# SyncE opens the first score level ahead of its loads of expert weights, and ScalarE takes a one-column exponential ahead of its wait for the level

## The chip, the core and the metric

The kernel runs on one NeuronCore of a Trainium2 chip. The core has five engines with an instruction stream each: TensorE (PE in the profile; its weight loads are PEld), VectorE (DVE), ScalarE (ACT), GpSimd (POOL) and SyncE (SP), which here issues transfers. The engines meet only through semaphores. The metric is the device time of one execution in microseconds (us), the median of several runs. A second number is the span of the one execution that the hardware profiler recorded.

## The reference, cut to what matters

4096 rows of width 128 pass through four layers, each added to its input: an adjacency attention, a dense mixture of two experts, a second adjacency layer and a mixture of experts with a choice of two experts for each row. The change lies at the start of the third layer:

```python
h = jnp.tanh(input @ W + b)
inp = input @ W
e = (h @ a)[:, 0]
valid = jnp.sum(h, axis=1) != 0
mask = (adj[:M] > 0) & valid[None, :]
scores = jnp.where(mask, e[None, :], neg)
m = jnp.max(scores, axis=1, keepdims=True)
w = jnp.where(mask, jnp.exp(scores - m), 0.0)
att = w / jnp.maximum(jnp.sum(w, axis=1, keepdims=True), 1e-30)
return att @ inp
```

The fourth layer adds, for each row, the two best of eight experts of the form gelu(x W1 + b1) W2 + b2; their weights are the `weights` that the diff mentions.

## The kernel before, in words

There are four functions, `prepare`, `attend`, `mix_and_project` and `gather_and_route`, each with one block in which every engine has its own program. A block ends with a barrier of all five engines. The change lies in the last one, `gather_and_route`, whose block begins at L1381.

`mix_and_project` leaves in SBUF: the scores `e` (32 columns, one per tile of 128 rows), `valid`, the normalized rows `xn`, and `levels`, a number that VectorE works out at L1000 from the spread of the scores. Its last ScalarE instruction is a one-column exponential into a spare column (L1114).

`gather_and_route` computes exp(e - max) in levels: a row of the adjacency whose sum is too small at one level is taken at the next, with all scores lifted by 16. The body of a level is a loop of a runtime count: `levels` (L1366 to L1370) reads the count from SBUF into a register (`value_load`, L1368) and runs `Fori` over it (L1369). Each engine does that for itself. In the profiled execution the body runs once.

The body of a level, `level_of`, exists on each engine and begins with a wait for the semaphore `level_open` to reach the number of the level. SyncE raises `level_open` once ahead of its own `levels` (L1429), and once more at the end of each level (L1427), when all engines have reported that they are done.

- SyncE (L1383 on) first issues five transfers that bring all expert weights into `weights`: W1 (L1385), W2 in two (L1387), b2 (L1389), b1 (L1390). They signal `weights_in`, for which ScalarE waits ahead of the first expert tile (`step_of(0)`, L1644 on), and VectorE after the levels. Then it raises `level_open` (L1429) and enters `levels`. Inside the level its first work waits for `first_table`, which is written after five of the eight chunks.
- VectorE (L1903 on) waits for a column of ones from GpSimd, enters the loop, waits for the level, writes `exponent` (L1906), waits for ScalarE's exponential, scales it (L1913), and makes for each of eight groups `values` (L1769) and the low half of `parts` (L1775).
- ScalarE (L1657 on) waits for the level, then for `exponent`, writes `weight` with the exponential (L1661), and then for each group the high half of `parts` (L1605).
- TensorE waits for the level and then, in chunk 0, for `parts` of each group. Each of the eight chunks is 32 tiles of two matmuls of 512 columns (L1467), with small turns, gates and ranks between the groups.
- GpSimd blanks the ones column (L1701) and two parts of `rows` (L1703), waits for the level, and later scatters rows by indirect DMA (L1713).

The functions that read activation tables are Exp, Tanh and Gelu. The program loads a table in front of the instruction that needs it (ACT_TABLE_LOAD in the trace); the loop body holds an Exp at its beginning and Gelus at its end.

Of the kernel before, what the change touches and what calls it, by code (L numbers as in the profile page):

```python
# [16 lines left out]
ACT = mybir.ActivationFunctionType  # L17
AX = mybir.AxisListType

P = 128  # L20
# [1198 lines left out]
def gather_and_route(nc, io, sb, ps):  # L1219

    with ExitStack() as ctx:
        buf = lambda name, shape, dt=F32: ctx.enter_context(nc.sbuf_tensor(name, shape, dt))
# [10 lines left out]
        values = buf("values", [P, VALUE_SLOTS, SUB, D])  # L1233
        sumsT = buf("sumsT3", [P, GROUP])
        exponent, weight = buf("exponent", [P, TILES]), buf("weight", [P, TILES])
        take, inverse = (buf(n, [P, SUB])[:, :] for n in ("take", "inverse"))
        e, valid, xn, left = sb["e"], sb["valid"], sb["xn"], sb["left"]
        mask = sb["mask"][:, :].bitcast(F8)
# [29 lines left out]
        level_open, level_closed = sem("level_open"), sem("level_closed")  # L1268
# [98 lines left out]
        def levels(eng, body):  # L1367
            count_ = eng.value_load(sb["levels"][0:1, 0:1], min_val=1, max_val=MOST_LEVELS)  # L1368
            with eng.Fori(1, count_ + 1) as level:  # L1369
                body(level)  # L1370
# [3 lines left out]
        def landed_rows(level, chunks, u):  # L1374

            return (level - 1) * (PER_CHUNK * len(range(u, LAST, SLOTS))) + PER_CHUNK * len(range(u, chunks, SLOTS))
# [4 lines left out]
        with nc.Block() as block:  # L1381

            @block.sync  # L1383
            def _(sp):
                sp.dma_start(weights[:, :, 0:F], io["W1b"].rearrange("e d f -> d e f")).then_inc(weights_in, 16)  # L1385
                for f in range(FH):
                    sp.dma_start(weights[:, :, F + f * D:F + (f + 1) * D],  # L1387
                                 io["W2b"].rearrange("e (f p) d -> f p e d", p=P)[f]).then_inc(weights_in, 16)
                sp.dma_start(weights[:, :, 2 * F:2 * F + D], io["b2b"].partition_broadcast(P)).then_inc(weights_in, 16)  # L1389
                sp.dma_start(weights[:, :, 2 * F + D:], io["b1b"].rearrange("e p f -> p e f")).then_inc(weights_in, 16)  # L1390

                def load_rows(k, landed, before):
                    start = sp.value_load(table[0:1, 1, k:k + 1], min_val=0, max_val=E * N + (ROUTED_STEPS - 1) * 2 * P)  # L1393
                    if before:

                        sp.wait_ge(landed, 16 * before)
                    sp.dma_start(sorted_rows[:, k, :, :], io["sorted"][bass.ds(start, 2 * P), :].rearrange("(h p) n -> p h n", p=P))\  # L1397
                        .then_inc(landed, 16)

                def level_of(level):  # L1400
                    sp.wait_ge(level_open, level)
                    sp.sem_inc(entered, 1)
                    sp.wait_ge(first_table, 1)
                    for n in range(SLOTS):
                        sp.wait_ge(scattered[n], landed_rows(level, FIRST_CHUNKS, n))
                        sp.sem_inc(entered, 1)
                    for k in range(FIRST):
                        load_rows(k, rows_in[0][k % LOADS], k // LOADS)
                    sp.wait_ge(second_table, 1)
                    for n in range(SLOTS):  # L1410
                        sp.wait_ge(scattered[n], landed_rows(level, SECOND_CHUNKS, n))
                        sp.sem_inc(entered, 1)
                    for k in range(FIRST, EARLY):
                        load_rows(k, rows_in[0][k % LOADS], k // LOADS)

                    for n in range(SLOTS):
                        sp.wait_ge(scattered[n], landed_rows(level, LAST, n))
                        sp.sem_inc(entered, 1)
                    for u in range(OUTS[0]):
                        sp.wait_ge(y_out[0][u], level * (32 * len(range(u, FIRST, OUTS[0]))))  # L1420
                        sp.sem_inc(entered, 1)
                    for done in level_done.values():
                        sp.wait_ge(done, level)
                        sp.sem_inc(level_closed, 1)
                    for spent in each_level:
                        sp.sem_clear(spent)
                    sp.sem_inc(level_open, 1)  # L1427

                sp.sem_inc(level_open, 1)  # L1429
                levels(sp, level_of)  # L1430

                sp.wait_ge(last_scattered, PER_CHUNK)
                sp.wait_ge(rest_table, 1)
                for k in range(EARLY, ROUTED_STEPS):
                    load_rows(k, rows_in[1][(k - EARLY) % LOADS], (k - EARLY) // LOADS)
                for u in range(OUTS[1]):
                    sp.wait_ge(y_out[1][u], 32 * len(range(u, ROUTED_STEPS - FIRST, OUTS[1])))
                for g in range(GROUPS):
                    u = g % RING
                    if g >= RING:  # L1440
                        sp.wait_ge(mixed_added, g - RING + 1)
                    sp.dma_start(both[:, u, :, :, :], io["mixed"][2 * g * GROUP:2 * (g + 1) * GROUP, :].rearrange("(p c s) d -> p c s d", p=P, c=2))\
                        .then_inc(both_in[u], 16)
                    if g >= RING - 1:
                        store = g - RING + 1
                        sp.wait_ge(mixed_added, store + 1)
                        sp.dma_start(io["out"].rearrange("(t p) d -> p t d", p=P)[:, store * SUB:(store + 1) * SUB, :],
                                     x_tiles[:, store * SUB:(store + 1) * SUB, :]).then_inc(rows_out, 16)
                for store in range(GROUPS - RING + 1, GROUPS):
                    sp.wait_ge(mixed_added, store + 1)  # L1450
                    sp.dma_start(io["out"].rearrange("(t p) d -> p t d", p=P)[:, store * SUB:(store + 1) * SUB, :],
                                 x_tiles[:, store * SUB:(store + 1) * SUB, :]).then_inc(rows_out, 16)
                sp.wait_ge(rows_out, 16 * GROUPS)
# [147 lines left out]
            def _(act):  # L1601

                def keep_high(g):
                    act.wait_ge(values_ready, g + 1)
                    nc.scalar.activation(parts[:, g * SUB:(g + 1) * SUB, 0, :], values[:, g % VALUE_SLOTS, :, :], ACT.Copy,  # L1605
                                         scale=1.0 / PART_SCALE).then_inc(hi_ready, 1)
# [14 lines left out]
                def keep_turned():  # L1621
                    return nc.scalar.activation(xT[:, :], ps[:, TURN_BANK, :], ACT.Copy)
# [30 lines left out]
                def steps(c, *groups):  # L1653
                    for i in steps_at(c, *groups):
                        step_of(i)

                def level_of(level):  # L1657
                    act.wait_ge(level_open, level)
                    act.sem_inc(entered, 1)
                    act.wait_ge(exponent_ready, 1)  # L1660
                    nc.scalar.activation(weight[:, :], exponent[:, :], ACT.Exp).then_inc(exp_ready, 1)  # L1661
                    for g in range(GROUPS):
                        keep_high(g)
                    for c in range(GROUPS):
                        scale_low_sums(c)
                        steps(c + 1, 0, 1, 2)
                        if c == LAST:
                            break
                        act.wait_ge(turned, c + 1)
                        if c:  # L1670

                            act.wait_ge(gates_ready, c)
                        keep_turned().then_inc(xT_ready, 1)
                        steps(c + 1, 3, 4)
                        act.wait_ge(measured, c + 1)
                        if c >= SLOTS:

                            act.wait_ge(scattered[c % SLOTS], landed_rows(level, c, c % SLOTS))
                        stage(c, 0).then_inc(staged, 1)
                        steps(c + 1, 5)  # L1680
                        stage(c, 1).then_inc(staged_again, 1)
                        steps(c + 1, 6, 7)
                    act.wait_ge(staged_again, LAST)
                    act.wait_ge(down_ready[0], FIRST)
                    act.wait_ge(scattered[LAST % SLOTS], landed_rows(level, LAST, LAST % SLOTS))
                    act.sem_inc(level_done["act"], 1)
# [366 lines left out]
```

## Time and profile before

| what | value |
|---|---|
| median of 3 runs | 844.4 us (842.9 to 844.82) |
| the profiled execution's own time | 846.05 us |
| its span | 844.3 us |
| TensorE busy | 703.9 us (83% of the span) |
| VectorE busy | 571.5 us (68%) |
| ScalarE busy | 498.9 us (59%) |
| GpSimd busy | 196.8 us (23%) |
| mean granted TensorE clock | 0.924 of full speed |

Times in rows are us from the start of the span, durations of single instructions in ns. An engine's name with a q (SPq, ACTq) is its sequencer: register, branch, semaphore and DMA-issuing instructions, which are not counted as busy. PEclk is the granted TensorE clock as a share of full speed, 0.50 at 1.2 GHz and 1.00 at 2.4 GHz.

### The profile page before, as it was taken

The page shows a single profiled execution, that of the slowest core. Times are in us where ns is not written, and L with a number is a line of the kernel's source. Part 1 is how long each engine was busy: PE and PEld are TensorE (multiplying, and loading weights), DVE is VectorE, ACT ScalarE, POOL GpSimd, SP SyncE. Part 2 cuts the span into 40 slices and gives each one's busy share as a digit, 9 for nine tenths or more (in the row PEclk, how much of TensorE's full clock was granted, in tenths as well). Part 3 has the DMA queues.
Part 4 walks back from the last instruction along what each step waited for, and adds up shares of the span by engine and source line. Part 5 has one row for each costly group of instructions (what it writes and reads, how often), then busy time and mean ns, then how long its engine had stood idle before and what let it go on. Part 6 is the DMA issues. An engine that isn't in the chain of part 4 may idle for free. (4 is left out here: it accounts for less than half of the span.)

```text
span 844.3 us, 11438 instructions
## 1 busy us (share of the span) xinstructions
PE 703.9 (83%) x3373; PEld 415.8 (49%) x3373; DVE 571.5 (68%) x1680; ACT 498.9 (59%) x751; POOL 196.8 (23%) x233
## 2 busy tenths in 40 slices
PE   1847999999999999999992997839999997759900
PEld 1643444444444444444442896615555674659900
DVE  7785577878787878788777388754566636646605
ACT  1745788888888888888873778531223452314400
POOL 2340000000000000000000544000455466477770
PEclk9979999999999999999995999869999998679965
DMA  4207999989999999998843000050011313136108
GB/s 131 75 0 205 275 269 243 274 242 281 236 285 245 276 255 266 256 261 239 225 126 135 4 1 2 0 126 1 26 40 39 91 42 82 41 89 150 41 24 299
DMA packets 100893, 124.58 MB, mean 148 GB/s; under 512 B 9038, under 2 KB 78930, under 8 KB 100576
## 3 DMA queue, kind: packets, MB, share of 16 engines
q1 hardware_dynamic: 96288, 115.32, 49.6%
q0 software_dynamic: 4544, 8.54, 3.1%
q8 instruction: 27, 0.44, 0.2%
q14 instruction: 34, 0.28, 0.1%
HBM read 88.54 MB, written 36.20 MB: 148 GB/s over the span
## 5 line engine op out<-in xcount | busy, mean ns | idle before, releaser
L564 DVE SCALAR_TENSOR_TENSOR probs<-adj,probs 128x1024 f32<-128x1024 int32 x128 | 156.8, 1225 | 79.1 <-ACT probs L537 68.8
L487 PE MATMUL ps<-x,qT 128*128 128x512 f16 x768 | 189.3, 384 | 3.2 <-PEq L205 3.2
L537 ACT ACTIVATE probs<-ps 128x1024 f32<-128x1024 f32 x128 | 131.1, 1024 | 52.2 <-PE ps L487 52.2
L548 ACT ACTIVATE mask<-probs 128x1024 fp8e4<-128x1024 f32 x128 | 134.0, 1047 | 0.0
L1467 PE MATMUL ps<-mask,parts 128*128 128x512 fp8e4 x512 | 118.4, 385 | 15.9 <-DVE parts L1775 15.9
L499 PE MATMUL ps<-probs,v 128*128 128x512 f32 x256 | 130.9, 593 | 0.0
L487 PEld LDWEIGHTS ps<-x,qT 128*128 128x128 f16 x768 | 75.8, 99 | 95.6 <-issue 7.0
L787 POOL MEMSET hT<- 128x128 f32 x1 | 0.2, 204 | 380.7 <-POOLq L440 380.7
L570 DVE TENSOR_TENSOR p_lo<-probs,p_hi 128x512 f16<-128x512 f32 x128 | 87.6, 684 | 0.1
L1733 POOL DMA_INDIRECT mixed_spill<-mask x78 | 76.8, 985 | 38.1 <-issue 20.6
L1467 PEld LDWEIGHTS ps<-mask,parts 128*128 128x128 f16 x512 | 50.2, 100 | 70.0 <-DVE parts L1775 15.9
L1713 POOL DMA_INDIRECT sorted_rows_spill<-rows,slots x64 | 63.2, 987 | 84.1 <-issue 54.3
L545 ACT ACTIVATE p_hi<-probs 128x512 f16<-128x512 f32 x128 | 79.6, 622 | 2.2 <-DVE probs L564 2.2
L1630 ACT ACTIVATE mask<-ps,mask 128x256 f32<-128x256 f32 x78 | 32.7, 470 | 61.8 <-PE ps L1523 61.8
L499 PEld LDWEIGHTS ps<-probs,v 128*128 128x128 f32 x256 | 48.4, 191 | 17.5 <-issue 0.3
L504 PE MATMUL ps<-p_lo,v 128*128 128x512 f16 x128 | 48.8, 381 | 3.1 <-DVE p_lo L570 3.0
L501 PE MATMUL ps<-p_hi,v 128*128 128x512 f16 x128 | 48.5, 379 | 0.0
L502 PE MATMUL ps<-p_hi,v 128*128 128x512 f16 x128 | 48.5, 379 | 0.0
L1523 PE MATMUL ps<-mask 128*128 128x256 f32 x156 | 44.6, 412 | 1.2 <-DVE mask L1884 1.2
L1534 PEld LDWEIGHTS ps<-mask 128*128 128x128 f32 x312 | 43.2, 201 | 2.8 <-ACT mask L1630 0.2
L1534 PE MATMUL ps<-mask 128*128 128x128 f32 x312 | 43.4, 284 | 0.0
L1892 DVE TENSOR_TENSOR mask<-ps,mask 128x256 f32<-128x256 f32 x39 | 16.6, 425 | 28.7 <-PE ps L1534 18.8
(290 smaller groups left out, 962.4 us busy)
## 6 DMA issues: line engine op xcount, KB each, us to landing
adj<-in_adj SPq DMA_DIRECT2D x128, 512.0 KB, 5.5
sorted_rows_spill<-blank SPq DMA_DIRECT2D x32, 528.0 KB, 7.3
sorted_rows_spill<-blank SPq DMA_DIRECT2D x26, 198.0 KB, 8.0
mask<-sorted_rows_spill SPq DMA_DIRECT2D x39, 132.0 KB, 2.6
xn<-mixed_spill SPq DMA_DIRECT2D x8, 512.0 KB, 5.7
mask<-in_x SPq DMA_DIRECT2D x4, 512.0 KB, 5.8
feat_spill<-mask SPq DMA_DIRECT2D x8, 256.0 KB, 2.0
x_feat<-in_x SPq DMA_DIRECT2D x8, 256.0 KB, 5.4
```

The costliest lines, as they stand in the source:

```text
L487: ins = nc.tensor.matmul(out, qT[:, q_half, j], kT[:, c, k_half * GROUP:(k_half + 1) * GROUP], start=(n == 0), stop=(n == 2))
L499: nc.tensor.matmul(out, v32[:, jp, :], probs[:, k % RING, 0:GROUP], start=(jp == 0), stop=False)
L504: nc.tensor.matmul(out, v16[:, jp, 0, :], p_lo[:, u, :], start=False, stop=(jp == PAIRS - 1))\
L537: nc.scalar.activation(probs[:, k % RING, :], ps[:, b:b + 2, :].rearrange("p b n -> p (b n)"), ACT.Exp, scale=1.0 / QK_SCALE ** 2).then_in ...
L545: nc.scalar.activation(p_hi[:, k % SLOTS, :], probs[:, k % RING, GROUP:], ACT.Copy).then_inc(hi_ready, 1)
L548: nc.scalar.activation(mask[:, k * W:(k + 1) * W], probs[:, k % RING, :], ACT.Sign, saturate=False).then_inc(mask_kept, 1)
L564: nc.vector.scalar_tensor_tensor(out=probs[:, k % RING, :], in0=adj[:, k % LOADS, :], scalar=0.0, in1=probs[:, k % RING, :], op0=ALU.is_gt ...
L570: nc.vector.tensor_tensor(p_lo[:, k % SLOTS, :], probs[:, k % RING, GROUP:], p_hi[:, k % SLOTS, :], ALU.subtract)\
L1467: ins = nc.tensor.matmul(sums_bank(c, part), parts[:, t, part, :], mask[:, (c * TILES + t) * GROUP:(c * TILES + t + 1) * GROUP], start=(t ...
L1534: ins = nc.tensor.matmul(down_out(k)[:, h * D:(h + 1) * D], hT[:, k % SLOTS, f, h * P:(h + 1) * P], current[:, k % WEIGHTS, F + f * D:F + ...
L1713: nc.gpsimd.indirect_dma_start(out=io["sorted"][:, :], out_offset=bass.IndirectOffsetOnAxis(ap=slots[:, n, t:t + 1].bitcast(U32), axis=0), ...
L1733: nc.gpsimd.indirect_dma_start(out=io["mixed"][:, :], out_offset=bass.IndirectOffsetOnAxis(ap=sorted_rows[:, k, h, D:D + 1].bitcast(U32), ...
```

## The change

SyncE's one increment of `level_open` ahead of `levels` moves from behind its five transfers to ahead of them. ScalarE takes, at the beginning of the loop body and ahead of its wait for the level, an exponential of the first column of the identity matrix into a new buffer `spare` of 128 partitions by one column, which nothing reads.

```diff
@@ gather_and_route
         exponent, weight = buf("exponent", [P, TILES]), buf("weight", [P, TILES])
+        spare = buf("spare", [P, 1])
         take, inverse = (buf(n, [P, SUB])[:, :] for n in ("take", "inverse"))
@@ SyncE's program
             def _(sp):
+                sp.sem_inc(level_open, 1)
                 sp.dma_start(weights[:, :, 0:F], io["W1b"].rearrange("e d f -> d e f")).then_inc(weights_in, 16)
@@
-                sp.sem_inc(level_open, 1)
                 levels(sp, level_of)
@@ ScalarE's program
                 def level_of(level):
+                    nc.scalar.activation(spare[:, :], sb["ident"][:, 0:1], ACT.Exp)
                     act.wait_ge(level_open, level)
                     act.sem_inc(entered, 1)
                     act.wait_ge(exponent_ready, 1)
                     nc.scalar.activation(weight[:, :], exponent[:, :], ACT.Exp).then_inc(exp_ready, 1)
```

## Rows read from the trace of the kernel before

**Rows 1.** Waits, 548 to 575 us: waiter, releaser, us in total, times, longest.

```profile
PE ps L1467 <- DVE parts L1775: 15.9, 1, 15.9
...
ACT L1661 <- SPq L1429: 11.6, 1, 11.6
DVE exponent L1906 <- SPq L1429: 8.6, 1, 8.6
```

**Rows 2.** Chain that ended last, 530 to 582 us: start us, us, what.

```profile
549.96 0.38 SPq L1385
...
555.95 1.65 SPq L1390
...
557.64 0.02 SPq L1429
...
557.75 1.28 ACT L1661
...
559.05 0.24 ACT weight L1661
...
560.92 0.70 DVE parts L1775
...
561.67 19.20 PE ps L1467 x80
```

**Rows 3.** L1368: durations ns min/median/max, first and last start us.

```profile
L1368 ACTq TENSOR_LOAD <-levels x1: 295/295/295, 550.0 to 550.0; - x1
...
L1368 DVEq TENSOR_LOAD <-levels x1: 332/332/332, 550.2 to 550.2; - x1
...
L1368 DVEq FUSED_REGOPS  x1: 190/190/190, 550.5 to 550.5; - x1
```

**Rows 4.** L1369, the entry of the loop, same columns.

```profile
L1369 ACTq MOVE  x2: 34/36/38, 550.5 to 550.6; - x2
L1369 DVEq MOVE  x2: 43/48/52, 550.8 to 550.9; - x2
```

**Rows 5.** Timeline, 545 to 562 us: start, us, engine, line, what, idle before.

```profile
544.70 1.28 ACT L1114 ACT_TABLE_LOAD   x1
...
545.99 0.20 ACT L1114 ACTIVATE w_all<-w_all 128x1 f32<-128x1 f32 x1
...
557.69 0.24 DVE L1906 TENSOR_SCALAR exponent<-e,lift 128x32 f32<-128x32 f32 x1 [8.64 <-SPq L1429]
```

**Rows 6.** Busy time by stretch: us, PE, PEld, DVE, ACT, POOL, PEclk, DMA share, GB/s.

```profile
546.00:550.00 4.00, 0.00 (x0) 0.00 (x0) 2.19 (x15) 0.19 (x1) 0.41 (x2) 0.78 0.00 0
...
558.00:560.00 2.00, 0.00 (x0) 0.00 (x0) 0.95 (x5) 1.27 (x2) 0.03 (x1) 0.50 1.22 279
...
562.00:565.00 3.00, 3.00 (x8) 1.06 (x7) 2.93 (x6) 1.26 (x2) 0.00 (x0) 0.50 0.00 0
565.00:566.00 1.00, 1.00 (x5) 0.45 (x4) 0.96 (x2) 0.63 (x1) 0.00 (x0) 0.86 0.00 0
...
466.00:468.00 2.00, 2.00 (x12) 1.66 (x11) 2.00 (x2) 1.70 (x3) 2.00 (x2) 0.93 0.08 17
...
757.00:760.00 3.00, 3.00 (x13) 2.70 (x12) 1.26 (x3) 0.26 (x1) 2.10 (x3) 0.53 0.68 177
...
600.00:644.00 44.00, 44.00 (x238) 23.57 (x237) 27.38 (x172) 13.14 (x30) 21.34 (x25) 1.00 0.11 35
```

**Rows 7.** Timeline of TensorE: two other starts after a pause.

```profile
461.59 0.79 PE L1145 MATMUL ps<-xT_hi,w_pair_lo 128*128 128x512 f32 x1 [3.91 <-DVE w_pair_lo L887]
...
753.99 0.69 PE L1513 MATMUL ps<-ident,mask 128*128 128x128 f32 x2 [9.25 <-DMA mask<-sorted_rows_spill]
```

**Rows 8.** Instructions on the tile `weight`, durations as in rows 3.

```profile
L1769 DVE TENSOR_TENSOR values<-xn,weight x8: 685/692/692, 559.5 to 568.3; 128x512 f32<-128x512 f32 x8
```

**Rows 9.** Instructions on the tile `weights`, durations as in rows 3.

```profile
L1879 DVE COPY mask<-weights x30: 495/497/729, 721.0 to 799.4; 128x642 f32 x30
L1639 ACT ACTIVATE mask<-weights x9: 737/738/740, 658.1 to 689.4; 128x642 f32 x9
```

## The prediction

> **What bounds the kernel now.** I read the page's chain of waits first: TensorE leads it, mostly with the gather matmuls of L1467 (80 of them in one piece, [rows 2]). Then I asked how each stage begins, since a change at a block's start can only move a start. The list of waits around the last block [rows 1] shows the reader one gap of 15.9 us in front of L1467, and behind it three engines that stand still for one semaphore: ScalarE 11.6 us and VectorE 8.6 us, both until SyncE's L1429. The chain of that stretch [rows 2] says what SyncE does meanwhile: it issues transfers from 549.96 to 557.6 us, and only then raises `level_open`, at 557.64. That is 557.64 - 549.96 = 7.68 us in which nobody computes, and they are on the path: every later step of the chain hangs on that increment (table load 557.75, exponential 559.05, first `parts` 560.92, first matmul 561.67). Behind it TensorE has no idle time (44.00 us busy of 44.00 between 600 and 644, [rows 6]), so the whole level moves with its first matmul.
>
> **The increment, moved.** It now comes at 549.96 instead of 557.64. It is SyncE's first instruction, so the five transfers go out later by one semaphore instruction, 0.02 us [rows 2]. Nothing waits for them soon: the queues are quiet from 562 on [rows 6], and the first reader of `weights` is at 658.1 [rows 9], which would move to about 651. SyncE's own entry into the loop stays behind the transfers and does not matter, since its first work in the level waits for a table written after five chunks.
>
> What is late next is the engines' own way in, which had been hidden in the 7.68 us. Each reads the level count into a register and sets up its loop. VectorE starts that at 550.2 (behind GpSimd's ones column), with 332 ns for the load and 190 ns for the register operation [rows 3], and has its last loop instruction at 550.9 [rows 4]; so `exponent` (0.24 us, [rows 5]) is written from about 551.0 to 551.2. ScalarE starts at 550.0 and has its last loop instruction at 550.6, of some 0.04 us [rows 3, 4]. It is the later one, because a table load of 1.28 us stands in front of its exponential [rows 2].
>
> **The spare exponential, added.** Before, the load began 0.1 us after the increment, since the load too stands behind the wait. In the new kernel it stands in front of the spare exponential, ahead of the wait, and begins at 550.6 + 0.04 + about 0.05 = 550.7. It ends at 551.97. Then comes the spare exponential itself, priced by the one-column exponential of L1114: 0.20 us, 0.01 us behind its load [rows 5]. So ScalarE is free at 552.18, a microsecond after `exponent` is ready, and the real exponential starts there. It started at 559.05 [rows 2]; the path is shorter by 559.05 - 552.18 = 6.87 us.
>
> I price the spare exponential at a loss of 0.20 us, not at nothing: with the level opened first, the load without it would also begin at 550.7, so it hides nothing of the load, and no other work covers it. If it were free the sum would be 7.1 us; if it cost the 0.24 us of the real one, 6.8 us. Only if the increment stayed behind the transfers would it be worth something by itself, the 1.28 us of the load.
>
> One thing here is decided by where loads are put. L1114 had already loaded a table and used Exp, and still L1661 loads again [rows 5, 2], because the loop body also ends in Gelus. So the first Exp of the body has the load, and a second Exp right behind it should find its table. The Trainium skill, "ScalarE: Activation LUTs", section "What ACT_TABLE_LOAD costs", puts a switch at about 1283 ns for the load and 1380 ns more for a drain. The load's 1.28 us agrees with the trace, but the drain is not seen here: at L1661 the exponential starts as the load ends. By the page's full price in both kernels the sum would be the same; with the drain in the new one alone it is the rival below.
>
> **From the first `parts` on.** The steps between the exponential and the first matmul keep their lengths, 561.67 - 559.05 = 2.62 us [rows 2]. They now lie under the weight transfers. The eight `values` of L1769 took 685 to 692 ns [rows 8], the first of them while the DMA engines were at 1.22 of their share and the later ones with none [rows 6], so 1% is what the burst cost. I take zero. The far end is the widest spread that any VectorE instruction on these weights shows, 495 to 729 ns, or 47% [rows 9]: on three steps of about 0.7 us that is 1.0 us, and on VectorE's pace of some 1.4 us per group against TensorE's 1.73 us (eight matmuls of 216 ns) it would cost 0.3 us in each of seven groups, 3 us in all. GpSimd's waits for the level go the same way and cost nothing.
>
> **The clock.** TensorE's granted clock fell to 1.2 GHz at 548.2 us (0.78 over 546 to 550), before the change's first instruction, so the restart is cold in both kernels. Before, it was at 2.4 GHz again at 565.3 (0.86 over 565 to 566): 3.6 us after the first matmul at 561.67, which costs half of that, 1.8 us [rows 2, 6]. Two other restarts took longer: from 461.59 to 466.3 is 4.7 us, from 753.99 to 759.8 is 5.8 us [rows 6, 7]. I take 3.6 us again, as the nearest row (same matmuls, fully busy), and keep 5.8 us as the end, a loss of (5.8 - 3.6) / 2 = 1.1 us. The other end is a loss of none, as there is no row with a faster recovery; the later pauses (before 754 among them) may shift by about as much either way. The Trainium skill, "TensorE: Matmul & The Clock Gate", section "What's actually happening", says that the same kernel meets a different number of cold matmuls from run to run; the three stretches agree that it is no constant. A median over runs then moves by the path alone, which is the sum without this term.
>
> **The sum.** 7.68 us of opening, minus 0.6 us of loop entry that comes to light and 0.20 us for the spare exponential, gives 6.9 us (the two starts of the exponential give 6.87). The profiled execution would go from a span of 844.3 to 837.4 us and from its own 846.05 to 839.2 us. That execution was 1.65 us above the median of the runs shown, so the forecast for the median is 844.4 - 6.9 = 837.5 us.
>
> **The rivals.**
>
> *The load is dearer or comes twice.* If a load is put in front of both exponentials, the real one waits for 1.28 us more: 5.6 us instead of 6.9, 838.8 us. For it: L1114's load did not save L1661 from its own. Against: those two lie on two sides of a loop entry, these two are neighbours in one body. A drain of 1.4 us at the new load would give nearly the same, 838.9 us; against it, both loads that the rows show took 1.28 us with the exponential right behind them [rows 2, 5].
>
> *The transfers slow the way in.* As worked out, up to 3 us, so 840.5 us; half of it, 839.0, if only the first groups meet the burst. Against it stand the even durations of L1769.
>
> *The opening does not decide, and the gain is given back.* Something tied to the transfers, or a later pause that waits for a queue, would hold the end where it is: 844.4 us. For it: the tail after 705 us has stops of TensorE that end with a DMA. Against: those transfers are issued by what the level itself computed, so they move too. The change not doing what it says, the increment seen late although issued first, would look the same.
>
> *Slower: the first chunk stays cold.* Place: L1467 after 554.8 us. If the clock stayed at 1.2 GHz, each us of it would cost half. The gain is eaten when the cold stretch after the restart is 3.6 + 2 x 6.9 = 17.4 us, and at 20 us the kernel is 1.3 us slower, 845.7 us. For it: the low stretch around the old start was 17.1 us long in all (548.2 to 565.3). Against: most of that was idle time, and no restart that is full of work took more than 5.8 us.
>
> **How the numbers follow.** Forecast 0.86; load 0.05; transfers 0.04; given back 0.03; cold 0.02. The predicted time is the forecast's, 837.5 us. The three runs before lie from 1.5 us under to 0.4 us over their median, which alone gives 836.0 to 837.9; the clock term adds 1.1 us on top, and the load rival reaches 838.9. Allowing a little under for the late pauses, 835.6 to 839.6 us. A measurement of this kernel can tell about 0.2%, 1.7 us, from no change. Faster by more than that is every case but the last two and part of nothing else: 0.95; within it 0.03; slower 0.02.
>
> **What would show it.** In the trace after, the semaphore instruction of `level_open` stands ahead of the five transfers; ScalarE's load begins near 550.7, the one-column exponential near 552.0, the real one near 552.2 with no load between; the first matmul is near 554.8 and the gap in front of L1467 falls from 15.9 to about 9.0 us. The distance from the first matmul to the end of the span, 844.3 - 561.67 = 282.6 us, should stay within about 1.5 us. I am wrong if a second load stands there, if `values` takes over 0.75 us, if the clock is still at 1.2 GHz 6 us after the first matmul, or if that distance grows by several us.

## The result, and the profile after

The changed kernel takes 837.44 us, the median of 5 runs (836.19 to 839.01). In the same comparison the kernel before took 844.82 us (5 runs, 842.9 to 846.21). The ratio is 0.9911 with a 95% interval of 0.9891 to 0.9931, a gain of 5.8 to 9.2 us. The forecast was 837.5 us in a range of 835.6 to 839.6. The profiled execution took 839.01 us with a span of 837.3.

The chain that ended last, 520 to 582 us of the changed kernel (start us, us, what), beside [rows 2]:

```profile
548.61 0.29 ACTq L1369
...
549.38 1.21 issue
550.59 0.20 ACT spare L1659
550.79 0.13 ACT weight L1663
...
550.94 0.20 DVE weight L1915
...
552.56 0.70 DVE parts L1777
...
553.31 20.16 PE ps L1468 x80
```

SyncE's issues are gone from the chain. It now begins with ScalarE reading the level count (L1369), and what the chain calls 1.21 us of issue is the end of the table load, as the timeline of the same stretch shows (start us, us, engine, line, what, idle before):

```profile
548.69 0.38 SPq L1387 DMA_DIRECT2D weights<-in_W1b  x1
...
549.29 1.28 ACT L1659 ACT_TABLE_LOAD   x1 [4.46 <-PEq L764]
549.62 0.24 DVE L1908 TENSOR_SCALAR exponent<-e,lift 128x32 f32<-128x32 f32 x1 [1.93 <-POOL xn L1703]
...
550.70 0.21 ACT L1663 ACTIVATE weight<-exponent 128x32 f32<-128x32 f32 x1
```

One load, none in front of the real exponential, and VectorE's `exponent` ready at 549.86, 0.8 us before ScalarE can use it. The waits of 548 to 575 us, beside [rows 1]:

```profile
PE ps L1468 <- DVE parts L1777: 8.8, 1, 8.8
...
ACT L1659 <- PEq L764: 4.5, 1, 4.5
```

The gap in front of the gather matmuls fell from 15.9 to 8.8 us. The busy time by stretch, columns as in [rows 6]:

```profile
557.00:558.00 1.00, 1.00 (x4) 0.33 (x3) 0.96 (x3) 0.30 (x2) 0.00 (x0) 0.50 1.20 291
558.00:559.00 1.00, 1.00 (x4) 0.39 (x3) 0.96 (x2) 0.63 (x1) 0.00 (x0) 0.58 1.14 190
559.00:560.00 1.00, 1.00 (x7) 0.47 (x5) 0.97 (x3) 0.63 (x1) 0.00 (x0) 1.00 0.26 25
```

The 0.58 over 558 to 559 puts the return to 2.4 GHz at 558.8 us, 5.5 us after the first gather matmul at 553.31; before it was 3.6 us.

Absolute times of the two traces can't be laid over one another, since the last block began at 549.96 us before and at 548.61 after, through the scatter of the code ahead of it, which is the same in both (over all thirteen traces below the block began between 546.4 and 550.3 us). So all distances below count from the block's start, taken at GpSimd's first memset (L1701 before, L1703 after). The account of the two profiled spans (844.3 - 837.26 = 7.04 us) is then:

| stretch | before | after | gained |
|---|---|---|---|
| start of the span to the block | 549.96 | 548.61 | 1.35 (scatter) |
| block to the real exponential | 9.09 | 2.09 | 7.00 |
| exponential to first gather matmul | 2.62 | 2.61 | 0.01 |
| first gather matmul to the first turn of sums | 19.04 | 20.00 | -0.96 |
| from there to the end | 263.59 | 263.95 | -0.36 |

### The profile page after: what moved, and what is told of

Read it like the earlier page. It is cut to its first block and busy times, and to the rows that moved or that the text cites. A ratio compares the mean times of both kernels' runs of the same rounds, so it can differ in the third digit from the quotient of the medians.

```text
span 837.3 us, 11439 instructions
## 1 busy us (share of the span) xinstructions
PE 701.9 (84%) x3373; PEld 414.1 (49%) x3373; DVE 571.6 (68%) x1680; ACT 498.9 (60%) x752; POOL 197.1 (24%) x233
## 5 line engine op out<-in xcount | busy, mean ns | idle before, releaser
L1468 PE MATMUL ps<-mask,parts 128*128 128x512 fp8e4 x512 | 120.2, 389 | 8.8 <-DVE parts L1777 8.8
L1623 ACT ACTIVATE xT<-ps 128x512 f32<-128x512 f32 x8 | 4.8, 597 | 51.8 <-PE ps L1486 51.8
```

Of the source, the lines that this page charges most:

```text
L1468: ins = nc.tensor.matmul(sums_bank(c, part), parts[:, t, part, :], mask[:, (c * TILES + t) * GROUP:(c * TILES + t + 1) * GROUP], start=(t ...
```

## The experiments

There were eleven more runs, e1 to e11: eight kernels with an edit of their own (e11 repeats e5), and the changed kernel twice more (e7 and e10). Each was timed beside the kernel before on its own chip, whose medians there were 844.63 us (e1, e2, e4, e5), 843.72 (e3, e6, e7, e8) and 845.66 (e9, e10, e11). "In" is the distance in us from the block's start to the real exponential and to the first gather matmul; "80 matmuls" is from the first gather matmul to the first turn of sums.

| kernel | median us (runs) | ratio, 95% interval | in | 80 matmuls |
|---|---|---|---|---|
| before | 844.82 (5) | 1 | 9.09, 11.71 | 19.04 |
| the change | 837.44 (5) | 0.9891 to 0.9931 | 2.09, 4.70 | 20.00 |
| e1 increment alone | 837.2 (4) | 0.9887 to 0.9925 | 2.07, 4.69 | 18.63 |
| e2 spare alone | 844.73 (10) | 0.9983 to 1.0011 | 7.70, 10.33 | 18.91 |
| e3 increment after W2 | 839.78 (1) | - | 2.69, 5.32 | 20.23 |
| e4 increment after b2 | 841.76 (4) | 0.9935 to 0.9968 | 6.24, 8.87 | 19.14 |
| e5 warm | 835.3 (5) | 0.9875 to 0.9912 | 2.09, 4.70 | 17.28 |
| e6 transfers late | 837.37 (4) | 0.9906 to 0.9946 | 2.09, 4.70 | 18.95 |
| e7 the change again | 836.27 (4) | 0.9886 to 0.9921 | 2.10, 4.70 | 19.96 |
| e8 warm twice | 835.33 (6) | 0.9886 to 0.9923 | 2.09, 4.70 | 17.28 |
| e9 warm, no spare | 834.98 (4) | 0.9857 to 0.9894 | 2.06, 4.69 | 17.28 |
| e10 the change, third | 838.78 (6) | 0.9894 to 0.9936 | 2.10, 4.70 | 20.01 |
| e11 warm again | 834.98 (5) | 0.9865 to 0.9898 | 2.09, 4.70 | 17.28 |

**e1_open_only.** The change without its second half.

```diff
-        spare = buf("spare", [P, 1])
...
-                    nc.scalar.activation(spare[:, :], sb["ident"][:, 0:1], ACT.Exp)
```

> The increment alone: level_open is raised ahead of the five transfers, ScalarE has no spare exponential. Distances are taken from the start of the last block (GpSimd's first memset on xn) to the start of the real exponential: 9.09 us before, 2.09 us after the change. Theory (the increment does it all, the spare hides nothing): ScalarE's load begins about 0.7 us into the block as in the changed kernel, the real exponential starts at 1.98 us, 0.1 us earlier than with the spare, and the time is that of the changed kernel, about 7 us under before. Rival (the spare exponential carries part of the gain by hiding the 1.28 us load): the exponential starts at 3.3 us and the gain is about 5.7 us.

Timeline of ScalarE, 544 to 555 us; its block began at 550.34:

```profile
551.11 1.28 ACT L1661 ACT_TABLE_LOAD   x1 [4.50 <-SPq L1385]
552.41 0.23 ACT L1661 ACTIVATE weight<-exponent 128x32 f32<-128x32 f32 x1
```

The load starts 0.77 us into the block and the exponential at 2.07, 0.02 us earlier than in the changed kernel and not 0.1: without the spare the load stands behind the wait for the level and the semaphore instruction after it, and starts 0.08 us later (0.77 against 0.69; e9, without the spare too, has 0.77 again). The time is that of the change. The spare exponential carries none of the gain.

**e2_spare_only.** The other half alone.

```diff
             def _(sp):
-                sp.sem_inc(level_open, 1)
...
+                sp.sem_inc(level_open, 1)
                 levels(sp, level_of)
```

> The spare exponential alone: the increment stays behind the five transfers. Theory: the load now lies in the 7.7 us in which all wait, so the real exponential follows VectorE's exponent directly: it starts at about 7.97 us from the block's start instead of 9.09, a gain of 1.1 us. Rival (a second load is placed in front of the real exponential, or the load is not on the path): 9.1 us and no gain. Together with the increment alone the two gains would add to 8.1 us if they were independent; the theory says that they are not, since the whole change gave 7.0.

Chain of 546 to 577 us:

```profile
554.64 0.02 SPq L1430
...
554.68 0.24 DVE exponent L1908
...
555.45 0.70 DVE values L1771
...
557.59 19.07 PE ps L1468 x80
```

The load is off the chain, and the real exponential starts 7.70 us into the block instead of 9.09. A part of the 1.39 us is not the spare's: the five issues took 7.39 us here against 7.68 before. Relative to the increment the exponential moved from 1.41 us behind it (557.64 to 559.05) to 0.32 behind (554.64 to 554.96), so the spare is worth 1.1 us, as expected. The time does not show it: 844.73 against 844.63 us, and the interval of the ratio ends at 0.9983, 1.4 us. A gain of 1.1 us is just inside; whether it is given back later can't be read from that, and stays open.

So on the way to the exponential the two halves do not add: 7.0 us for the increment, 1.1 for the spare alone, 7.0 together.

**e4_open_after_b2.** A dose between the two.

```diff
             def _(sp):
-                sp.sem_inc(level_open, 1)
...
+                sp.sem_inc(level_open, 1)
                 sp.dma_start(weights[:, :, 2 * F + D:], io["b1b"].rearrange("e p f -> p e f")).then_inc(weights_in, 16)
```

> The changed kernel with the increment put behind four of the five transfers (W1, W2 twice, b2), ahead of b1. Theory (the path follows the increment one to one wherever it is later than ScalarE's own way in, which ends 2.1 us into the block): the increment comes when the four issues are done, 5.99 us into the block in the trace of before, the real exponential 0.3 us later at 6.3 us, and the gain against before is 9.09 - 6.3 = 2.8 us. Rival (what counts is the load or the first transfers, not the increment): the exponential starts near 2.1 us and the gain is that of the changed kernel, 7 us.

Chain of 549 to 575 us; the block began at 549.52:

```profile
551.22 4.18 SPq L1390
...
555.44 0.02 SPq L1391
...
555.48 0.24 DVE exponent L1908
```

The exponential starts at 6.24 us, 0.3 us behind the increment, and the gain is 2.9 us by the medians and 2.85 by the traces (9.09 - 6.24). With e2 and e3 this is the line that the theory drew: exponential = increment + 0.3 us, down to ScalarE's own way in.

**e3_open_after_w2.** The same with the increment ahead of the transfer of b2, timed once.

> The changed kernel with the increment behind three of the five transfers (W1 and the two of W2), some 2.2 us into the block. Theory: this is where VectorE's exponent becomes the later of the two inputs, by a little: exponent ready at about 2.45 us, the real exponential at 2.5 us against 2.09, so 0.4 us of the gain is lost. If the issues of W2 are slower, as in the profile after, the exponential is later by the same amount, and always 0.27 us behind the increment. Rival (each issue ahead of the increment costs its whole duration): 2.2 us lost.

Chain of 548 to 555 us; the block began at 548.43:

```profile
549.48 1.28 SPq L1388
...
550.80 0.02 SPq L1390
...
550.85 0.24 DVE exponent L1908
```

The second issue of W2 took 1.28 us, so the increment came at 2.37 and the exponential at 2.69 us, 0.6 us later than in the change and not 2.4. By the same line an increment up to 2.09 - 0.3 = 1.8 us into the block costs nothing, since ScalarE is not there yet; no run placed one just there. The time does not follow the way in here: that is 6.4 us shorter than before (9.09 - 2.69), and the one execution took only 3.9 us less than the median of before. Of the 2.5 us between the two, 1.2 are the clock, since its stretch at 1.2 GHz after the first matmul was the longest of all traces, 6.0 us against 3.6. The rest is less than the 3 to 5 us over which single executions of one kernel scatter, and stays open.

**e6_transfers_late.** The changed kernel without the burst under the way in.

```diff
                 sp.sem_inc(level_open, 1)
+                sp.wait_ge(parts_ready, GROUPS)
                 sp.dma_start(weights[:, :, 0:F], io["W1b"].rearrange("e d f -> d e f")).then_inc(weights_in, 16)
```

> The changed kernel, but SyncE waits for the last parts of the first chunk before it issues the five transfers, so that the whole way in and VectorE's eight groups run with quiet queues. Theory (the transfers cost the way in nothing): the first gather matmul stays 4.70 us from the block's start, values at 0.69 us each, and the time is that of the changed kernel. Rival (the burst slows the way in, which hid part of the gain): the first matmul comes earlier than 4.5 us, or the groups get shorter. What stays to be seen: the weights then land some 14 us later, long before their reader, about 100 us into the block.

Instructions on the tile `weight`, first of this kernel, then of the changed one (durations ns min/median/max, first and last start us):

```profile
L1772 DVE TENSOR_TENSOR values<-xn,weight x8: 684/692/693, 550.8 to 559.6; 128x512 f32<-128x512 f32 x8
```

```profile
L1771 DVE TENSOR_TENSOR values<-xn,weight x8: 687/692/692, 551.2 to 559.9; 128x512 f32<-128x512 f32 x8
```

With quiet queues or under a full burst the way in is 4.70 us and `values` take 692 ns. The transfers slow nothing there, to the precision of the trace. The time, 837.37 us, is 6.4 us under before on the same chip, against 7.5 for the changed kernel (e7), which is within the scatter of the two.

**e7_after_again and e10_after_third.** No edit.

> The changed kernel once more, on the same chip as the other runs of this call. Theory: the path from the block's start to the first gather matmul repeats to 0.05 us (4.70), while the stretch at 1.2 GHz behind it differs from run to run (5.6 us in the profile after, 3.3 to 3.9 in three others), so that the 80 matmuls of L1468 take between 18.6 and 20.7 us. Rival (the 5.6 us belong to the changed kernel, as a consequence of its shorter pause): 20.0 us again. The time: 7 us under before.

> The changed kernel, on the same chip as the two with added matmuls. 836.3 to 837.4 us by the earlier medians, 7 to 7.4 us under before, and 4.70 us from the block's start to the first gather matmul.

The way in repeated to 0.01 us. The time of e7 was 7.5 us under before, as expected; that of e10, 838.78 us, lay 1.4 us above its expected range, and 6.9 us under the kernel before on the same chip. The 80 matmuls took 19.96 and 20.01 us, so the 20.0 us that the rival of e7 named came each time: in all three traces of the changed kernel the clock returned 10.2 to 10.3 us into the block, 5.5 to 5.6 us after the first matmul. But e1 and e6, which have the same pause of 8.8 us and the same way in, returned after 2.8 and 3.4 us. So neither the length of the pause nor the point of the restart fixes it. The windows of e6 around the return, its first matmul being at 552.97:

```profile
556.00:557.00 1.00, 1.00 (x5) 0.40 (x4) 0.96 (x3) 0.63 (x1) 0.00 (x0) 0.80 0.00 0
557.00:559.00 2.00, 2.00 (x11) 0.91 (x10) 1.97 (x4) 0.65 (x2) 0.00 (x0) 1.00 0.00 0
```

What does differ among these five is where in the pause the clock fell. The window of its fall in the changed kernel (`after`), whose last matmul ahead of the pause ended at 544.5 us:

```profile
545.00:546.00 1.00, 0.00 (x0) 0.00 (x0) 0.83 (x6) 0.00 (x0) 0.00 (x0) 0.60 0.00 0
```

and the windows of the fall and the return in e1, whose last matmul ended at 546.2 us and whose first gather matmul is at 555.03:

```profile
547.00:548.00 1.00, 0.00 (x0) 0.00 (x0) 0.57 (x4) 0.00 (x0) 0.22 (x1) 0.79 0.00 0
557.00:558.00 1.00, 1.00 (x4) 0.40 (x3) 0.96 (x3) 0.63 (x1) 0.00 (x0) 0.59 1.22 293
```

In the three traces of the changed kernel the clock fell 0.7 us after that last matmul and stayed low for 13.6 to 13.7 us. In e1 and e6 it fell after 1.4 and 2.0 us and stayed low for 10.2 us. Why it falls earlier in one execution than in another no run shows.

**e5_warm and e11_warm_again.** The changed kernel with matmuls that nothing reads, into a free PSUM bank, over TensorE's pause.

```diff
                 score(GROUPS // 2 - 1)
+                for _ in range(56):
+                    nc.tensor.matmul(ps[:, COLUMN_BANK + 1, 0:P], before[:, :], ones_of[:, :], start=True, stop=True)
...
+                def warm(n):
+                    for _ in range(n):
+                        nc.tensor.matmul(ps[:, 7, 0:P], before[:, :], ones[:, :], start=True, stop=True)
...
                     pe.sem_inc(entered, 1)
+                    warm(40)
...
+                warm(12)
                 levels(pe, level_of)
```

> The changed kernel plus matmuls of 128 columns that nothing reads, to keep TensorE at work over its pause: 56 behind the last score of the third stage, 12 at the entry of the last block, 40 behind the wait for the level. Theory (what the change leaves behind in front of L1468 is a cold restart, 5.6 us at 1.2 GHz in the profile after, worth 2.8 us): the granted clock stays at 2.4 GHz over the pause, the 80 matmuls of L1468 take 17.3 us instead of 20.2, and the time is 2 to 3 us under the changed kernel, about 835. Rival (the added matmuls delay the barrier or the first gather matmul by as much as the clock gives back): no difference to the changed kernel. A second rival: the clock falls all the same, and the 80 matmuls take 19 to 20 us.

> The kernel of e5_warm once more beside the changed one. Theory (the warm start is worth half of a stretch at 1.2 GHz that was 2.8 to 6.1 us long in the traces so far, so 1.4 to 3 us): 834.8 us, 2 us under the changed kernel of this call, and 80 matmuls in 17.3 us. Rival (the first median of 835.3 was a lucky draw within the scatter of 3 to 5 us that every kernel has): no difference.

The busy time by stretch in e5, columns as in [rows 6], and then its chain of 546 to 572 us:

```profile
544.00:548.00 4.00, 2.96 (x54) 2.81 (x52) 1.94 (x13) 0.00 (x0) 0.60 (x4) 1.00 0.01 2
548.00:552.00 4.00, 2.92 (x50) 2.60 (x47) 2.49 (x9) 2.67 (x5) 0.20 (x1) 1.00 0.73 218
552.00:556.00 4.00, 3.65 (x17) 1.67 (x18) 3.90 (x7) 1.72 (x4) 0.00 (x0) 1.00 1.16 303
```

```profile
552.35 17.44 PE ps L1470 x80
```

The clock stays at 2.4 GHz, the way in stays at 4.70 us, and the 80 matmuls take 17.28 us instead of 20.0: 2.7 us. Side by side on one chip the medians are 834.98 us (5 runs, 834.03 to 835.81) and 838.78 (6 runs of the changed kernel, 834.76 to 839.8): 3.8 us. The trace accounts for 2.7 of them, and the ranges overlap. On another chip the kernel with the filler and a second one (e8) was only 0.9 us under the changed kernel (835.33 against 836.27, e7), so what the filler is worth in the median is known no better than 1 to 4 us.

**e9_warm_no_spare.** The same without the spare exponential and its buffer.

> The same without the spare exponential. Theory: the traces with and without the spare had the first gather matmul at 4.70 and 4.69 us, since the second exponential starts 0.1 us behind the first, so the time is that of e11_warm_again within the scatter. Rival (the spare matters once the clock is warm): a start later than 4.8 us.

834.98 us and 4.69 us: as expected, no difference. This is the fastest kernel of the study, beside e11: ratio to before 0.9876 (0.9857 to 0.9894).

**e8_warm_twice.** e5 with a second filler, in the pause of the expert tiles.

```diff
+                    if k + 2 == EARLY:
+                        for _ in range(140):
+                            nc.tensor.matmul(ps[:, 4, 0:P], before[:, :], ones[:, :], start=True, stop=True)
                     if k + 2 < ROUTED_STEPS:
                         turn_rows(k + 2)
```

> The kernel with the added matmuls at the level's start (e5_warm) plus 140 of 128 columns ahead of TensorE's wait for the rows of the last chunk, the pause of about 9 us in the expert tiles. Theory (that pause costs a cold restart of 5 to 6 us too): the low stretch there goes, the time is 2 to 3 us under e5_warm, about 9.5 + 2.5 = 12 us under before. Rival (TensorE is not what decides in the expert tiles, where VectorE and ScalarE pass on each tile, so a faster clock is waited away): no difference to e5_warm, which was 1.07% under before.

Timeline of TensorE, 728 to 752 us:

```profile
732.30 7.98 PE L1602 MATMUL ps<-ones,before 128*128 128x128 bf16 x140
741.14 0.44 PE L1516 MATMUL ps<-ident,mask 128*128 128x128 f32 x2 [0.87 <-DMA mask<-sorted_rows_spill]
741.42 1.03 PE L1526 MATMUL ps<-mask 128*128 128x256 f32 x4
```

The restart is warm, at 741.14 us, the same time as in e5, where the first four matmuls of 256 columns (L1526) took 1.91 us instead of 1.03. The last VectorE step of the expert tiles starts at 787.84 us instead of 789.49, 1.65 us earlier. And yet the end does not move. The chains of e8 and then of e5 in their last stretch:

```profile
807.04 0.97 POOL mixed_spill L1746
808.32 2.08 DMA mixed_spill<-mask
```

```profile
806.72 0.97 POOL mixed_spill L1743
807.99 2.08 DMA mixed_spill<-mask
```

GpSimd's scatters follow one another every 1.28 us, and the last one is no earlier in e8 (808.32 us) than in e5 (807.99): the time won on TensorE is waited away in GpSimd's queue. The median is 8.4 us under before (835.33 against 843.72), where e5 was 9.3. The forecast of 12 us under before was wrong; the rival of no difference was right, but with GpSimd and not VectorE or ScalarE as the engine that holds the end.

## Why the prediction was right

The total was right, and so was its main step, the increment. Two of the small terms were off: the spare exponential, priced at 0.20 us, costs 0.02, and the clock, taken as unchanged, took 1.0 us in the profiled execution.

**The increment.** Priced at 7.68 us of opening less 0.6 us of loop entry. The trace gives 7.00 us from the block to the exponential, against a forecast of 6.87. e1 shows the whole gain with the increment alone, and e2, e3 and e4 follow the increment one to one until ScalarE's way in takes over. The way in was read off the row of registers that the wait had covered [rows 3, 4]: the load was to start 0.74 us into the block, and started at 0.69. Moving the increment to the front delayed the first transfer by 0.08 us (548.69 - 548.61) and not by the 0.02 of the instruction alone; the first reader of `weights` starts at 650.7 us, so nothing waits for it.

**The spare exponential.** Priced at a loss of 0.20 us, its duration in [rows 5]. It cost less: the real one starts 0.11 us behind it (550.59 to 550.70), since the two overlap, and in whole kernels the difference is 0.02 us (2.09 against 2.07 in e1). That term should have been the distance of two starts and not the duration of one, less the 0.08 us by which the load itself starts earlier in front of the spare. The Trainium skill, "ScalarE: Activation LUTs", section "What ACT_TABLE_LOAD costs", states an overlap of about 93 ns for ACTIVATEs back to back; the trace agrees (203 ns long, starts 0.11 us apart, so 0.09 us of overlap). The sign was right, that it hides nothing once the level opens first, and e2 shows the one case in which it does.

**The load.** One, of 1.28 us, with the exponential 0.02 us behind it: neither the second load nor the drain. The rivals at 838.8 and 838.9 us are refuted.

**The burst.** Taken as nothing; e6 removes it and finds nothing: the median of `values` is 692 ns with and without it. The 1% that I laid to the burst, 685 to 692 ns, is there with quiet queues too (684 to 693).

**The clock.** This is the term that was mis-sized in the profile: I took 3.6 us again and named 5.8 us as the far end; the three traces of the changed kernel have 5.5 to 5.6, 1.0 us of loss (the -0.96 of the table). Over nine traces without filler, before among them, the return came 2.8 to 6.0 us after the first matmul, so a faster recovery than 3.6 us exists (2.8 in e1), and the other end of the term was not a loss of none but a gain of 0.4 us. The cold rival, a stretch beyond 17.4 us, did not appear. There is one trace of the kernel before, so whether the medians carry this 1.0 us is not shown. The Trainium skill, "TensorE: Matmul & The Clock Gate", section "What's actually happening", expects the number of cold matmuls to differ from run to run; across kernels with an equal way in the traces agree (2.8, 3.4, 5.5 us), while the three of the one kernel do not show it.

**The rest.** From the first matmul to the end I expected 282.6 us within 1.5; it is 283.95, of which 0.96 is the clock just named. Little was given back: the pause in the expert tiles, which ends with a transfer, ended 204.03 us into the block before (753.99 - 549.96) and 198.13 after (746.74 - 548.61), 5.90 us earlier, where 7.01 of way in less 0.96 of clock leave 6.05. The remaining 0.36 us is not traced further. That the profiled span (837.3) met the forecast (837.4) so closely is luck, as the table shows: 1.35 us of scatter ahead of the block stand against 1.32 us of clock and tail. That the median (837.44) met its forecast (837.5) is partly luck as well: the forecast went out from 844.4 us, and in the comparison the kernel before took 844.82. The medians of the three sets of runs of the changed kernel lie 7.4, 7.5 and 6.9 us under before; with an interval of 5.8 to 9.2 us on the first they bear out about 7 us, and can't tell 6.9 from 7.4 or see a term of 0.2 us.

## What to carry to other kernels

A semaphore that opens a stage should be raised ahead of the transfers that its engine issues, if the stage does not need them: an issue costs its engine time, and whoever stands behind it in the program pays for all of them. Before pricing such a gain at the whole wait, look at what the waiting engines did in it (registers, table loads), since that comes to light next. Two changes that shorten the same wait need not add, and one of them may be worth nothing once the other is made; measure each alone.

## What the runs showed of the hardware that I had not expected

- An issue of a transfer has no fixed length: that of b2 (512 KB in packets of 512 bytes) took 3.75 us before, 3.35 after and between 3.27 (e3) and 5.07 (e7) over thirteen traces; that of b1 (8 KB in pieces of 8 bytes) 1.59 (e4) to 2.85 (after). Issues cannot be placed to a tenth of a us.
- Filling a pause of 9 us with 108 small matmuls kept TensorE's granted clock at 2.4 GHz in all four traces that have them (e5, e8, e9, e11), though TensorE was idle for a quarter of the time (2.96 us busy of 4 and 2.92 of 4 in e5). It delayed neither the barrier (the block began 4.1 us after the last real matmul, as without them) nor the first gather matmul (4.70 us into the block).
- The same filler in front of a stretch that GpSimd's queue of indirect transfers decides (one every 1.28 us) bought nothing.
